# Layer 0 of a two-layer convolution kernel: half-row means from the wave sums, the base bank moved out by ScalarE, the virtual-row product as four tiles

## The chip, the cores and the metric

One core of one Trainium2 chip. The time is device microseconds of one execution, from the first instruction to the last with what lies around them. The kernel before took 4186.73 us in the median of three runs (4180.75 to 4187.25).

## The reference

The input x is (8, 16, 512, 512) in float32. Two layers follow one another.

```python
# layer 0
x = x + irfft2(conv3x3_complex(rfft2(group_norm(x))) + bias)   # 16 -> 16 channels, over the spectrum
# layer 1
x = x + box15x15(group_norm(x))                                # mean filter, per channel
```

The group norm takes mean and variance over two channels of one image (8 groups, eps 1e-5). A 3x3 convolution over a half spectrum becomes, back in the image domain, products of pointwise waves (cosine and sine of the column and of the row), channel mixes, and a term for the edge of the half spectrum, which is a Hilbert transform along the row. The kernel computes layer 0 in that form.

## The kernel before

The kernel works on one image after another (a hardware loop over seven, the eighth written behind it). An image lies in SBUF as `img`, 128 partitions (16 channels by 8 row blocks) by T = 64 rows of 512 columns. One *slot* handles one of the 64 rows `t`; the running row number over all images is `n`. Even and odd columns are two halves `a` of 256 (the parity); a bank of PSUM holds both halves.

Layer 0 of an image, slot by slot, four engines in a pipeline, each with its own program order and semaphores between them. SyncE only fetches the mixing matrices of a later row (`bd_all`, `wrap_mat`) once `p0_ready` says that their buffer is free. The rotation is over NG = 4 rows (`s`).

- **TensorE (PE)**, in slot n: `front_hilbert(n + 1)` (12 matmuls, printed as L442), `front_turn(n + 2)` (8 transposes, L432), `mix(n)`. `mix` runs 36 matmuls of 64x64 tiles by 512 columns (L557) in ten rounds. Row half 0 and row half 1 of the array work on different banks at the same time: `p1`, `p0[s]`, `p2`. In the first and the tenth round only one half of the array has work. Then comes one full 128x128 matmul by 512 columns into `p0[s]`, the virtual rows (`wrap_mat`, L601), whose end is `p0_ready`. Before `mix`, PE waits for `t1_done` of the row before (bank `p1` read), before round 1 for `t2_done`, before round 3 for `x1_done` of row n - 4 (bank `p0[s]` read).
- **ScalarE (ACT)**, in slot n: `normalise(n + 3)` in two instructions (L719 in f16, L720 in f32 into the single buffer `g32`), which waits for `p0_ready` of row n - 1; `keep_hilbert(n + 1)` (L734); `keep_turned(n + 2)` (L726); `add_half_row(n - 3)`: two instructions on 128x1 (L741) make the half-row correction `half_row` from `stat` and `known`, two on 128x256 (L747) add it to the row in place. Its end is `x1_whole`.
- **VectorE (DVE)**, in slot n: `wave_terms(n - 1)`, four SCALAR_TENSOR_TENSOR on 128x256, two from `p1` (L1065) and two from `p2` (L1071), each bank by a wave table into `term_row`; `low_hilbert(n + 1)` (L1038), which waits for ACT's L734; `finish_row(n - 2)`: one SCALAR_TENSOR_TENSOR from bank `p0[s]` and `q_row` into `img` (L1080), then BATCH_NORM_STATS of the row (L1083).
- **GpSimd (POOL)**, in slot n: `split_g(n + 3)` (L1194), which waits for ACT's L720; `add_terms(n - 1)`: L1201 adds the two wave terms, L1203 adds the old row, giving `q_row`. All three read two SBUF operands of 512 columns. In the slots 5 to 11 and 61 to 63 of an image `presum` adds one row more (L1214, L1217) for the box filter of layer 1; it waits for `x1_whole`. Four more presums follow the last row.

Why there is a half-row correction: the Hilbert term of a row leaves open the mean of its even and of its odd columns. The kernel before computes these means beforehand (`known`, from `kappa`, `block_mat`, `vmean`, `from_virtual`) in the head of layer 0 (L1027 to L1056 on DVE, L530 to L533 on PE), compares them with the means that BATCH_NORM_STATS finds, and adds half of the difference. At the end of the loop L1108 mends the statistics in the same way, and only then does `statistics` (L939) begin.

The head of layer 0 (lines 984 to 1056 on DVE) also makes `wrap_row` (L1043), the moving operand of the matmul of L601. It is ready at about the time when the first `mix` has done its 36 matmuls.

Layer 1 (the box filter) and the statistics of the next image follow; the change does not touch them.

## Time and profile before

| | |
|---|---|
| profiled execution, device time | 4181.21 us |
| its span | 4179.4 us |
| median of three runs | 4186.73 us |
| granted TensorE clock, mean | 0.954 |
| busy over the span | PE 88%, DVE 75%, ACT 63%, POOL 63% |
| chain that ended last, by engine | PE 61%, DVE 11%, POOL 10%, issue 6%, DMA 5%, SP queue 3%, ACT 3% |
| its costliest line | L557 (`mix`), 20% |

Busy times overlap, and a share over the span mixes layer 0 with layer 1. The chain says which engine was last at each step. PE instructions overlap one another, so PE is read by the distance from one start to the next and not by durations. The same holds for DVE: two instructions with no wait between them overlap by about 0.08 us.

### The profile page before, as it was taken

To read this page: it belongs to the slowest core of one execution; us is meant where nothing else is said; L and a number is where in the kernel's file an instruction comes from. 1 tells how busy PE (TensorE), PEld (TensorE's weight loads), DVE (VectorE), ACT (ScalarE), POOL (GpSimd) and SP (SyncE) were. 2 spreads that over 40 slices of the span, in tenths; PEclk is the share of its full clock that TensorE was granted. 3 is DMA by queue.
4 is the path that set the end of the run, shared out by engine and by line. 5 is a ranking of instruction groups with operands and counts; after the bars stand their busy time and mean duration, and the time that the engine had idled before them with its cause. 6 is when DMAs were issued, how large, how long until landed. Compare 5 with 4: busy or idle time off the path is not lost.

```text
span 4179.4 us, 122916 instructions
## 1 busy us (share of the span) xinstructions
PE 3686.3 (88%) x41104; PEld 2617.8 (63%) x41104; DVE 3141.1 (75%) x5894; ACT 2619.4 (63%) x4784; POOL 2633.4 (63%) x2177
## 2 busy tenths in 40 slices
PE   3199898998989989899898997899888998989988
PEld 1166575666756667566665666666575666756667
DVE  8778776787767878678776887778776787767876
ACT  0089822997249962599427993289822997239962
POOL 4078742886628865488546885378842887528865
PEclk8599998999999999999999999999999999999999
DMA  7411165111841128211381114711165111741114
GB/s 160 153 45 51 38 189 149 51 51 39 220 119 50 51 61 234 81 51 52 98 235 41 53 48 131 205 43 51 40 179 157 51 51 36 212 127 51 51 48 137
DMA packets 228317, 406.43 MB, mean 97 GB/s; under 512 B 98144, under 2 KB 173504, under 8 KB 215744
## 3 DMA queue, kind: packets, MB, share of 16 engines
q1 hardware_dynamic: 228032, 402.82, 34.8%
q8 instruction: 156, 2.56, 0.3%
q14 instruction: 129, 1.06, 0.1%
HBM read 255.78 MB, written 146.80 MB: 96 GB/s over the span
## 4 chain that ended last, share of the span: by engine, by line
PE 61%; DVE 11%; POOL 10%; issue 6%; DMA 5%; SPq 3%; ACT 3%; DVEq 0%; POOLq 0%; ACTq 0%
PE p L557 20%; PE h_ps L442 13%; PE h_ps L627 10%; DMA img<-in_x 5%; PE xt_ps L432 4%; PE p L653 4%; POOL ob_all L1201 3%; PE p L480 2%; PE h_ps L557 2%; POOL arena L1194 2%; PE p L601 2%; DVE stat L918 2%; POOL ob_all L1203 2%; POOL arena L1217 2%; DVE ob_all L1132 1%
## 5 line engine op out<-in xcount | busy, mean ns | idle before, releaser
L557 PE MATMUL p<-arena,bd_all 64*64 64x512 f16 x16896 | 1217.7, 379 | 16.8 <-DVE ob_all L1065 8.6
L1194 POOL TENSOR_TENSOR arena<-arena 128x512 f16<-128x512 f32 x512 | 592.9, 1158 | 599.1 <-ACT arena L720 531.4
L557 PEld LDWEIGHTS p<-arena,bd_all 64*64 64x64 f16 x16896 | 607.6, 105 | 386.9 <-issue 186.8
L700 ACT ACTIVATE arena<-h_ps 128x512 f16<-128x512 f32 x512 | 305.8, 597 | 861.7 <-PE h_ps L627 651.3
L1252 POOL TENSOR_TENSOR arena<-img 128x512 f32<-128x512 f32 x392 | 499.3, 1275 | 495.0 <-PE h_ps L627 467.0
L442 PE MATMUL h_ps<-hilbert,arena 128*128 128x256 f16 (+1 forms) x6240 | 781.2, 275 | 30.8 <-DVE arena L1038 21.9
L1203 POOL TENSOR_TENSOR ob_all<-ob_all,img 128x512 f32<-128x512 f32 x512 | 662.8, 1295 | 82.9 <-POOL ob_all L1201 72.9
L442 PEld LDWEIGHTS h_ps<-hilbert,arena 128*128 128x128 f16 x6240 | 610.2, 98 | 164.1 <-issue 24.5
L1201 POOL TENSOR_TENSOR ob_all<-ob_all 128x512 f32<-128x512 f32 x512 | 654.5, 1278 | 26.3 <-DVE ob_all L1071 26.3
L1038 DVE SCALAR_TENSOR_TENSOR arena<-h_ps,arena 128x512 f16<-128x512 f32 x512 | 354.0, 691 | 385.8 <-ACT arena L734 384.9
L627 PE MATMUL h_ps<-bd_all,arena 128*128 128x128 f32 x3584 | 543.1, 287 | 0.0
L627 PEld LDWEIGHTS h_ps<-bd_all,arena 128*128 128x128 f32 x3584 | 450.8, 192 | 122.1 <-issue 114.6
L747 ACT ACTIVATE img<-img,half_row (+1 forms) x1024 | 486.3, 526 | 62.2
L726 ACT ACTIVATE arena<-xt_ps 128x1024 f16<-128x1024 f16 x512 | 517.8, 1011 | 1.7 <-PE xt_ps L432 1.7
L719 ACT ACTIVATE arena<-img,sc 128x512 f16 (+1 forms) x512 | 442.3, 864 | 95.4 <-POOL arena L1194 29.5
L1116 DVE TENSOR_TENSOR arena<-h_ps,arena 128x512 f16<-128x512 f32 x512 | 352.8, 689 | 183.2 <-ACT arena L700 178.4
L1065 DVE SCALAR_TENSOR_TENSOR ob_all<-p,bias_c,cosw 128x256 f32<-128x256 f32 x1024 | 441.9, 473 | 11.2 <-PE p L557 10.8
L1071 DVE SCALAR_TENSOR_TENSOR ob_all<-p,bias_c,cosw 128x256 f32<-128x256 f32 x1024 | 443.7, 475 | 0.0
L720 ACT ACTIVATE arena<-img,sc 128x512 f32 (+1 forms) x512 | 433.3, 846 | 0.0
L480 PE MATMUL p<-img,bd_all 128*64 128x256 f32 x2048 | 325.7, 426 | 114.1 <-DMA img<-in_x 63.8
L653 PE MATMUL p<-band,arena 128*128 128x135 f16 (+1 forms) x4096 | 334.3, 225 | 79.6 <-DVE ob_all L1132 77.6
L1083 DVE BATCH_NORM_STATS2 stat<-img (+1 forms) x512 | 355.4, 694 | 62.0
(156 smaller groups left out, 4461.2 us busy)
## 6 DMA issues: line engine op xcount, KB each, us to landing
out<-ob_all SPq DMA_DIRECT2D x512, 256.0 KB, 3.2
img<-in_x SPq DMA_DIRECT2D x192, 512.0 KB, 6.4
bd_all<-bd_dram SPq DMA_DIRECT2D x512, 192.0 KB, 2.2
img<-in_x SPq DMA_DIRECT2D x128, 256.0 KB, 4.6
wrap_mat<-tab_wrap_h SPq DMA_DIRECT2D x512, 32.0 KB, 2.0
bd_dram<-ob_all SPq DMA_DIRECT2D x16, 768.0 KB, 3.5
arena<-tab_hilbert_kernel SPq DMA_DIRECT2D x8, 256.0 KB, 3.3
hilbert<-tab_hilbert SPq DMA_DIRECT2D x1, 522.0 KB, 4.0
```

What stands on the lines that cost most here:

```text
L442: m = mm(dst(a), xT[:, 4 * lx + k, 0:rows], tb["hilbert16"][:, lt, k, 0:cols], start=(half == 0 and i == 0), stop=(half == 1 and i == 2))
L557: m = mm(bank[out_half * HP:(out_half + 1) * HP, :], low(half, 6 * lm + (j if own else j + 1)), (g_part if own else h_part)(half, lp), sta ...
L627: m = mm(turned_ps[u % 2][:, k, :], row[:, k * P:(k + 1) * P], mat, start=(i == 0), stop=(i == len(terms) - 1))
L653: m = mm(p0[0][:, lo:hi], parts[u % 2][:, l, k, :], tb["band16"][:, lo - k * P + R:hi - k * P + R], start=(u == 0 and k == 0 and l == 0), ...
L719: nc.scalar.activation(halves(gp[s][:, 0, :]), row, ACT.Identity, bias=sc[:, 9:10], scale=sc[:, 8:9])
L726: nc.scalar.activation(xT.rearrange("p k (s m) -> p k s m", s=2)[:, :, ::-1, :], xt_ps[:].rearrange("p k (s m) -> p k s m", s=2), ACT.Iden ...
L747: ins = nc.scalar.activation(row, row, ACT.Identity, bias=half_row[:, s, a:a + 1])
L1071: ins = V.scalar_tensor_tensor(t2[:, a, :], p2[:, a * HALF:(a + 1) * HALF], bias_c[:, 0, t, 1 - a:2 - a], sinw[:, a, :], ALU.add, ALU.mult)
L1194: G.tensor_tensor(gp[s][:, 1, :], g32, gp[s][:, 0, :], ALU.subtract).then_inc(g_split, 1)
L1201: G.tensor_tensor(q, term_row[s % 2][0], term_row[s % 2][1], ALU.add).then_inc(t_added, 1)
L1203: G.tensor_tensor(q, q, parity(img[:, t, :]), ALU.add).then_inc(q_done, 1)
L1252: G.tensor_tensor(diff[u % 2], img[:, u + R, :], img[:, u - R - 1, :], ALU.subtract).then_inc(moved, 1)
```

## The change

- `mix` is put in another order. Row half 0 does `p0[s]`, then `p1`, then `p2`; row half 1 does `p1`, `p2`, `p0[s]`. The 128x128 matmul of the virtual rows becomes four 64x64 tiles (`wrap_terms`): two in round 3 on row half 0, two in round 9 on row half 1. There are now ten rounds of four matmuls and nothing behind them. The wait for the bank `p0[s]` stands at the start of `mix` (on `base_done`), the one for `t2_done` before round 3, the one for `v_wrap` (only in the first row) before round 3.
- The four wave instructions on DVE also write their sums along the row (`accum_out`, into `wave_sum`). A new function `half_sums` makes `half_mean` from them in two TENSOR_SCALAR on 128x1, in SBUF from SBUF; DVE does it behind `low_hilbert`.
- ACT does not touch the finished row any more. `keep_base(n - 2)`, now the first thing in its slot, moves bank `p0[s]` with scale and `half_mean` as bias into `base_row` in SBUF (two instructions on 128x256), waiting for `p0_ready`, `half_made` and `x1_done`.
- `finish_row` on DVE adds `q_row` and `base_row`, both in SBUF, by TENSOR_TENSOR, where it read PSUM before.
- `known`, `vmean`, `vwrap`, `half_row`, the table `from_virtual`, a third of `block_mat` and `c_tab`, the waits on them and the correction L1108 are gone. `presum` waits for `x1_done`.

```diff
+        base_row = [piece[8 + s].rearrange("p (a j) -> p a j", a=2) for s in range(2)]
...
-        block_mat = sb("block_mat", [P, 9, P])
+        block_mat = sb("block_mat", [P, 6, P])
         kappa = sb("kappa", [P, 3, T, 2])
         bias_c = sb("bias_c", [P, 2, T, 2])
-        known = sb("known", [P, T, 2])
-        half_row = sb("half_row", [P, NG, 2])
-        vmean = sb("vmean", [NV, 2])
-        vwrap = sb("vwrap", [P, 3, 2])
+        wave_sum = sb("wave_sum", [P, NG, 2, 2])
+        half_mean = sb("half_mean", [P, NG, 2])
...
-                pe.wait_ge(v_means, b + 1)
-                for j in range(3):
-                    m = mm(c_ps[:, 40 + 2 * j:42 + 2 * j], tb["from_virtual"][:, j, :], vmean[:], start=True, stop=True)
-                m.then_inc(v_meant, 1)
...
                     pe.wait_ge(t1_done, PRIMED + n)
+                    if first > 0:
+                        pe.wait_ge(base_done, PRIMED + n - (NG - 1))
                     pe.sem_inc(mix_step, 1)
-                    first_half = [(p1[:], 2)] * 3 + [(p0[s], 0)] * 3 + [(p2[:], 4)] * 3
+
+                    def wrap_terms(half, closes):
+                        for out_half in (half, 1 - half):
+                            m = mm(p0[s][out_half * HP:(out_half + 1) * HP, :],
+                                   wrap_mat[s][half * HP:(half + 1) * HP, out_half * HP:(out_half + 1) * HP],
+                                   wrap_row[half * HP:(half + 1) * HP, :], start=False, stop=closes,
+                                   skip_group_check=True)
+                        return m
                     for r in range(10):
-                        if r == 1:
-                            pe.wait_ge(t2_done, PRIMED + n)
-                            pe.sem_inc(mix_step, 1)
-                        if r == 3 and first > 0:
-                            pe.wait_ge(x1_done, PRIMED + n - (NG - 1))
-                            pe.sem_inc(mix_step, 1)
-                        if r < 9:
-                            bank, j = first_half[r]
-                            if r == 6:
-                                pe.wait_ge(p2_half, n + 1)
+                        if r < 3:
+                            m = half_terms(p0[s], 0, r, 0, True, False)
+                        elif r == 3:
+                            if first == 0 and s == 0:
+                                pe.wait_ge(v_wrap, b + 1)
                                 pe.sem_inc(mix_step, 1)
-                            m = half_terms(bank, j, r % 3, 0, r < 6, r >= 6)
-                            if r == 2:
-                                m.then_inc(p1_half, 1)
-                            if r == 5:
-                                m.then_inc(p0_half, 1)
-                            if r == 8:
-                                m.then_inc(p2_ready, 1)
-                        if r >= 1:
-                            bank, j = first_half[(r + 5) % 9]
+                            wrap_terms(0, False).then_inc(p0_half, 1)
+                        elif r < 7:
                             if r == 4:
                                 pe.wait_ge(p1_half, n + 1)
                                 pe.sem_inc(mix_step, 1)
+                            m = half_terms(p1[:], 2, r - 4, 0, False, True)
+                            if r == 6:
+                                m.then_inc(p1_ready, 1)
+                        else:
                             if r == 7:
+                                pe.wait_ge(p2_half, n + 1)
+                                pe.sem_inc(mix_step, 1)
+                            m = half_terms(p2[:], 4, r - 7, 0, False, True)
+                            if r == 9:
+                                m.then_inc(p2_ready, 1)
+                        if r < 3:
+                            m = half_terms(p1[:], 2, r, 1, True, False)
+                            if r == 2:
+                                m.then_inc(p1_half, 1)
+                        elif r < 6:
+                            if r == 3:
+                                pe.wait_ge(t2_done, PRIMED + n)
+                                pe.sem_inc(mix_step, 1)
+                            m = half_terms(p2[:], 4, r - 3, 1, True, False)
+                            if r == 5:
+                                m.then_inc(p2_half, 1)
+                        elif r < 9:
+                            if r == 6:
                                 pe.wait_ge(p0_half, n + 1)
                                 pe.sem_inc(mix_step, 1)
-                            m = half_terms(bank, j, (r - 1) % 3, 1, r <= 3, r > 3)
-                            if r == 3:
-                                m.then_inc(p2_half, 1)
-                            if r == 6:
-                                m.then_inc(p1_ready, 1)
-                    if first == 0 and s == 0:
-                        pe.wait_ge(v_wrap, b + 1)
-                    mm(p0[s], wrap_mat[s][:], wrap_row[:], start=False, stop=True, skip_group_check=True).then_inc(p0_ready, 1)
+                            half_terms(p0[s], 0, r - 6, 1, False, False)
+                        else:
+                            wrap_terms(1, True).then_inc(p0_ready, 1)
...
-                    if s == NG - 1:
-                        pe.wait_ge(known_made, b + 1)
...
-                def add_half_row(n, t, s):
-
-                    act.wait_ge(x1_counted, n + 1)
+                def keep_base(n, s):
+
+                    act.wait_ge(p0_ready, PRIMED + n + 1)
+                    act.wait_ge(half_made, n + 1)
+                    act.wait_ge(x1_done, PRIMED + n - 1)
                     for a in range(2):
-                        ins = nc.scalar.activation(half_row[:, s, a:a + 1], stat[:, t, 1 + 3 * a:2 + 3 * a], ACT.Identity,
-                                                   bias=known[:, t, a:a + 1], scale=-0.5)
-                    ins.then_inc(half_made, 1)
-                    act.wait_ge(half_made, n + 1)
-                    for a in range(2):
-                        row = img[:, t, a:W:2]
-                        ins = nc.scalar.activation(row, row, ACT.Identity, bias=half_row[:, s, a:a + 1])
-                    ins.then_inc(x1_whole, 1)
+                        ins = nc.scalar.activation(base_row[s % 2][:, a, :], p0[s][:, a * HALF:(a + 1) * HALF],
+                                                   ACT.Identity, bias=half_mean[:, s, a:a + 1], scale=unscale)
+                    ins.then_inc(base_done, 1)
...
+                    if t >= 2:
+                        keep_base(n - 2, (s + 2) % NG)
...
-                    if t >= 3:
-                        add_half_row(n - 3, i * NG + s - 3, (s + 1) % NG)
...
-                dve.wait_ge(v_rows, b + 1)
-                lk(V.tensor_reduce(vmean[:], vrow[0:NV], mybir.AxisListType.X, ALU.add))
-                V.tensor_scalar(vmean[:], vmean[:], 1.0 / HALF, None, ALU.mult).then_inc(v_means, 1)
                 dve.wait_ge(c_made, b + 1)
-                V.tensor_copy(bias_c[:], c_tab[:, 0:2])
-                lk(V.scalar_tensor_tensor(known[:], c_tab[:, 2], unscale, parity_mean, ALU.mult, ALU.add))
-                V.scalar_tensor_tensor(known[:, 0, 0:1], bcol[:, 0:1], 1.0 / HALF, known[:, 0, 0:1],
-                                       ALU.mult, ALU.add).then_inc(c_kept, 1)
+                V.tensor_copy(bias_c[:], c_tab).then_inc(c_kept, 1)
...
-                dve.wait_ge(v_meant, b + 1)
                 dve.wait_ge(c_kept, b + 1)
-                lk(V.tensor_copy(vwrap[:].rearrange("p j a -> p (j a)"), c_ps[:, 40:46]))
-                for f in range(2):
-                    for a in range(2):
-                        ins = V.scalar_tensor_tensor(known[:, :, a], tb["trig_h"][:, f], vwrap[:, 1 + f, a:a + 1],
-                                                     known[:, :, a], ALU.mult, ALU.add)
-                    lk(ins)
-                for a in range(2):
-                    ins = V.tensor_scalar(known[:, :, a], known[:, :, a], vwrap[:, 0, a:a + 1], 0.5, ALU.add, ALU.mult)
-                ins.then_inc(known_made, 1)
-                dve.wait_ge(known_made, b + 1)
...
                         ins = V.scalar_tensor_tensor(t1[:, a, :], p1[:, a * HALF:(a + 1) * HALF],
                                                      bias_c[:, 1, t, 1 - a:2 - a], cosw[:, a, :],
-                                                     ALU.subtract, ALU.mult)
+                                                     ALU.subtract, ALU.mult, accum_out=wave_sum[:, s, 0, a:a + 1])
...
-                                                     ALU.add, ALU.mult)
+                                                     ALU.add, ALU.mult, accum_out=wave_sum[:, s, 1, a:a + 1])
...
+                def half_sums(n, s):
+
+                    dve.wait_ge(t1_done, PRIMED + n + 1)
+                    dve.wait_ge(t2_done, PRIMED + n + 1)
+                    for a in range(2):
+                        ins = V.tensor_scalar(half_mean[:, s, a:a + 1], wave_sum[:, s, 0, a:a + 1],
+                                              wave_sum[:, s, 1, a:a + 1], -0.5 / HALF, ALU.add, ALU.mult)
+                    ins.then_inc(half_made, 1)
+
+                def finish_row(n, t, s):
 
                     dve.wait_ge(q_done, PRIMED + n + 1)
-                    dve.wait_ge(p0_ready, PRIMED + n + 1)
-                    V.scalar_tensor_tensor(parity(img[:, t, :]), halves(p0[s]), unscale, q_row[s % 2],
-                                           ALU.mult, ALU.add).then_inc(x1_done, 1)
+                    dve.wait_ge(base_done, PRIMED + n + 1)
+                    V.tensor_tensor(parity(img[:, t, :]), q_row[s % 2], base_row[s % 2], ALU.add).then_inc(x1_done, 1)
...
+                    if t >= 1:
+                        half_sums(n - 1, (s - 1) % NG)
                     if t >= 2:
-                        finish_row(n - 2, i * NG + s - 2, (s - 2) % NG, first - (s < 2))
+                        finish_row(n - 2, i * NG + s - 2, (s - 2) % NG)
...
-                for t in (T - 2, T - 1):
-                    finish_row(b * T + t, t, t % NG, T // NG)
-                dve.wait_ge(half_made, (b + 1) * T)
-                V.scalar_tensor_tensor(parity_mean, parity_mean, 0.5, known[:], ALU.mult, ALU.add).then_inc(stat_fixed, 1)
-                dve.wait_ge(stat_fixed, b + 1)
+                half_sums(b * T + T - 1, (T - 1) % NG)
+                for t in range(T - 2, T):
+                    finish_row(b * T + t, t, t % NG)
+                dve.wait_ge(x1_counted, (b + 1) * T)
                 statistics(b * 2 + 2, b)
...
-                    pool.wait_ge(x1_whole, n + 1)
+                    pool.wait_ge(x1_done, PRIMED + n + 1)
```

## Rows read from the trace of the kernel before

**Rows 1.** Windows: one stretch of the loop of layer 0, second image; window, length, busy time.

```profile
787.50:1000.10 212.60, 212.33 (x2694) 142.85 (x2691) 171.89 (x334) 203.53 (x378) 175.58 (x144) 1.00 0.18 51
```

**Rows 2.** Timeline: PE in one slot; start us, duration us, engine, line.

```profile
867.79 0.39 PE L601 MATMUL p<-wrap_row,wrap_mat 128*128 128x512 f16 x1
868.02 1.48 PE L442 MATMUL h_ps<-hilbert,arena 128*128 128x256 f16 x12
...
869.88 2.47 PE L557 MATMUL p<-arena,bd_all 64*64 64x512 f16 x36
...
872.28 0.39 PE L601 MATMUL p<-wrap_row,wrap_mat 128*128 128x512 f16 x1
```

**Rows 3.** Timeline: DVE in the same slot.

```profile
868.22 0.88 DVE L1065 SCALAR_TENSOR_TENSOR ob_all<-p,bias_c,cosw 128x256 f32<-128x256 f32 x2
...
869.01 0.87 DVE L1071 SCALAR_TENSOR_TENSOR ob_all<-p,bias_c,cosw 128x256 f32<-128x256 f32 x2
...
870.54 0.69 DVE L1038 SCALAR_TENSOR_TENSOR arena<-h_ps,arena 128x512 f16<-128x512 f32 x1 [0.67 <-ACT arena L734]
...
871.15 0.74 DVE L1080 SCALAR_TENSOR_TENSOR img<-p,sc,ob_all 128x512 f32 x1
...
872.04 0.69 DVE L1083 BATCH_NORM_STATS2 stat<-img  x1
...
872.65 0.86 DVE L1065 SCALAR_TENSOR_TENSOR ob_all<-p,bias_c,cosw 128x256 f32<-128x256 f32 x2
```

**Rows 4.** Timeline: ACT's `add_half_row` in the loop, and `virtual_base` in the head.

```profile
866.81 0.48 ACT L741 ACTIVATE half_row<-stat,known 128x1 f32 x2
...
867.43 0.95 ACT L747 ACTIVATE img<-img,half_row  x2
```
```profile
714.89 1.02 ACT L755 ACTIVATE ob_all<-p,edge,sc 128x256 f32<-128x256 f32 x2 [3.62 <-DVE edge L1016]
```

**Rows 5.** Timeline: POOL in the same slot.

```profile
870.11 1.16 POOL L1194 TENSOR_TENSOR arena<-arena 128x512 f16<-128x512 f32 x1 [0.62 <-ACT arena L720]
...
871.23 1.28 POOL L1201 TENSOR_TENSOR ob_all<-ob_all 128x512 f32<-128x512 f32 x1
...
872.70 1.29 POOL L1203 TENSOR_TENSOR ob_all<-ob_all,img 128x512 f32<-128x512 f32 x1 [0.19 <-POOL ob_all L1201]
```

**Rows 6.** Timeline: two small DVE instructions, no wait between them.

```profile
696.62 0.14 DVE L966 TENSOR_SCALAR sc<-sc 128x1 f32<-128x1 f32 x1
696.68 0.14 DVE L967 TENSOR_SCALAR sc<-sc 128x1 f32<-128x1 f32 x1
```

**Rows 7.** Timeline: DVE and POOL in the setup, then one DVE instruction behind layer 0.

```profile
27.42 1.22 DVE L310 TENSOR_TENSOR img<-img 128x1024 f32<-128x1024 f32 x1
...
33.83 3.25 DVE L308 TENSOR_TENSOR img<-img 128x1024 f32<-128x1024 f32 x1
```
```profile
32.68 3.33 POOL L308 TENSOR_TENSOR img<-img 128x1024 f32<-128x1024 f32 x1
```
```profile
1025.37 1.23 DVE L1138 TENSOR_SCALAR mean_in<-c_mask,sc 128x16 f32<-128x16 f32 x1
```

**Rows 8.** Timeline: POOL in two slots with a presum; starts of `mix` of rows 2 and 15.

```profile
754.65 1.29 POOL L1203 TENSOR_TENSOR ob_all<-ob_all,img 128x512 f32<-128x512 f32 x1
...
759.61 1.30 POOL L1203 TENSOR_TENSOR ob_all<-ob_all,img 128x512 f32<-128x512 f32 x1
```
```profile
733.55 2.47 PE L557 MATMUL p<-arena,bd_all 64*64 64x512 f16 x36
```
```profile
793.54 2.47 PE L557 MATMUL p<-arena,bd_all 64*64 64x512 f16 x36
```

**Rows 9.** Timeline: PE's two waits in the head of layer 0.

```profile
720.29 1.48 PE L442 MATMUL h_ps<-hilbert,arena 128*128 128x256 f16 x12 [0.67 <-DVE arena L1038]
...
727.21 1.48 PE L442 MATMUL h_ps<-hilbert,arena 128*128 128x256 f16 x12 [2.08 <-DVE arena L1038]
```

**Rows 10.** Timeline: DVE's last correction of layer 0.

```profile
1017.20 0.69 DVE L1108 SCALAR_TENSOR_TENSOR stat<-stat,known 128x128 f32<-128x128 f32 x1 [0.55 <-ACT half_row L741]
```

29 lines of the change are left out of this document (12 added, 17 removed).

## The prediction

> **What bounds the kernel now.** I read the chain that ended last first (the table ahead): PE 61%, its costliest line the mix. Then the windows: over 212.60 us of the loop of layer 0 PE is busy for 212.33, ACT for 203.53, POOL for 175.58 and DVE for 171.89 [rows 1]. So inside layer 0 PE sets the pace, and ACT is hardly behind. Then the timeline of one slot. PE's rows abut: from one L601 to the next are 4.49 us (867.79 to 872.28), and no PE row carries a wait [rows 2]. Eight images of 64 slots make 512 slots, so 0.01 us of a slot are 5 us of the time.
>
> DVE has to be read by starts. L1065 takes 0.79 us to the next start, L1071 the same (two of one kind), L1038 0.61 (870.54 to 871.15), L1080 0.89 with the gap behind it (871.15 to 872.04), L1083 0.61 (872.04 to 872.65): 3.69 us, and 0.67 us of the slot it waits for ACT's L734 [rows 3]. POOL has L1194, L1201, a gap of 0.19 and L1203, 3.88 us, and waits 0.62 for ACT [rows 5].
>
> **The change, part by part.**
>
> *The virtual-row product.* L601 takes 0.23 us of PE to the next start (867.79 to 868.02) [rows 2]. Its four tiles fill the empty places of rounds 0 and 9. The ten rounds stay (869.88 to 872.28 is 2.40 us, with the hand-over to the 128x128 array), so the slot becomes 4.49 - 0.23 = 4.26 us. Bounds: 0.23 gained, or nothing, if 40 matmuls take 40/36 of 2.40 us (0.27 more). I take the gain: round by round the array streams 512 columns, and a round with two matmuls does not start its successor sooner than one with four. In slots 2 to 63: 62 x 0.23 = 14.3 us per image. The price is that every other engine must do its slot in 4.26.
>
> *ACT.* The 128x1 pair L741 and the gap behind it go (0.62 us, 866.81 to 867.43), the pair L747 goes (0.95), and a pair from PSUM comes, between 0.95 (L747) and 1.02 us (L755) [rows 4]. ACT had 203.53/212.60 x 4.49 = 4.30 us of work and gets about 3.7 (3.9 with the gap counted). It fits. `keep_base` stands ahead of `normalise`, which PE and POOL wait for, but in the time in which ACT would wait for `p0_ready` of the row before. Its own wait, `half_made`, comes from DVE behind L1038; that is the one place where DVE can now hold up ACT.
>
> *DVE.* Out: L1080 from PSUM, 0.74. In: TENSOR_TENSOR of two SBUF rows, 0.69 by L1083's and L1038's length [rows 3], -0.05. Four accumulator outputs: no row shows one. Below, they cost nothing; above, one small instruction each with its whole 0.14 us (0.56). I take 0.06 each, the distance of small instructions with no wait [rows 6], 0.24. `half_sums`: two such, 0.13. Sum 3.69 - 0.05 + 0.24 + 0.13 = 4.01 of 4.26. It fits, with 0.25 us left, where it had 0.80.
>
> *The SBUF reads of DVE and POOL.* This is the part that the diff does not show. Now no DVE instruction of the slot has two full rows of 512 columns from SBUF while POOL runs [rows 3]. The setup shows what happens then. L310 on 128x1024 takes 1.22 us alone. L308, the same instruction, takes 3.25 (33.83 to 37.08) while POOL's L308 runs from 32.68 to 36.01; 36.01 + 1.07 (1024 columns at 1.22 us less start-up) is 37.08, to the hundredth [rows 7]. So DVE stood until POOL's instruction had ended. The Trainium skill says so too ("SBUF — State Buffer", "Who interferes with whom": two SBUF inputs on VectorE against a GpSimd read, an exclusive lock), and the trace agrees. The new TENSOR_TENSOR on 512 columns holds the reads for half of 1.07, 0.53 us, and waits for whatever POOL is in, 0 to 1.2 us. POOL's 3.88 becomes at worst 4.41; where DVE falls into POOL's own gap of 0.19 or its wait for ACT (0.27 of a 4.26 us slot), POOL loses less than 0.4 and stays within 4.26. DVE can wait at most 0.25 us before it sets the pace. I take it that the two settle in step, DVE in POOL's pauses, since each one that comes late is then met by a pause: 4.26 us. The other case is a rival.
>
> *Presums.* In their seven slots POOL needs 4.96 us (754.65 to 759.61). PE loses only 1.6 us to that now: rows 2 to 15 are 59.99 us apart, against 13 x 4.49 = 58.37 [rows 8]. Wanted were 7 x 0.47 = 3.3; a reserve of 1.7 covered the rest. After: 4.96 + 0.53 = 5.49 against 4.26, 7 x 1.23 = 8.6, less the reserve, 6.9. That gives back 5.3; with POOL's thinner reserve in faster slots I take 6.5.
>
> *Head.* PE waits 0.67 and 2.08 us for L1038, which stands behind the work on `known` [rows 9]. That work is gone. The new wait for `v_wrap` before round 3 costs PE about 1.9 us in row 0, as `wrap_row` is ready only when the 36 matmuls are done, but PE had 2.08 to wait there. The next Hilbert matmuls follow that mix at once. From the chain of starts: 0.9 us at each place, -1.8.
>
> *Tail.* L1108 and the wait for L741 ahead of it go: 0.69 + 0.55 = -1.2 [rows 10]. But the last TENSOR_TENSOR meets POOL's presums (+1 us), as do the small two-operand instructions of the statistics (+0.5), and POOL itself comes 0.5 later. +0.8 in sum, between -1.2 and +2.
>
> *Setup* is 1 us shorter (three of nine block matrices, one table). The SP queue waits for `p0_ready` as before.
>
> **Sum** per image: -14.3 + 6.5 - 1.8 + 0.8 = -8.8; I round the doubtful give-back up to -7.8. Eight images: -62, and the setup: 4181.2 - 63 = 4118 us for an execution like the profiled one. The median of the runs lies 5.5 above that one and the lowest 0.5 below, so the median may read as much higher: 4120.
>
> **The rivals.**
>
> *H, the two 128x1 instructions are held too (slower).* `half_sums` is TENSOR_SCALAR from SBUF to SBUF with one tensor operand. Such an instruction can be held as well: L1138, 128x16, takes 1.23 us beside a POOL instruction, where a small one takes 0.14 [rows 6, 7]. For it: same kind, same place. Against it: no row shows a 128x1 one beside POOL, so one element may be too few for the mode that does it. If it holds, DVE stands for one whole POOL instruction between the first and the second (POOL's next is already waiting), about 1.1 us of 1.27 [rows 5]: 4.01 + 1.1 = 5.1 us a slot, against 4.49 now. It decides as soon as the held time is over 0.25 us. 62 x 0.6 = 37, presum slots +2, head and tail -1: +38 x 8 = +305, 4490 us (4440 to 4560). The Trainium skill ("Vector Engine (DVE) Microarchitecture Reference", "5.1 Performance modes") lets an odd count use both ports if source and destination match; by that rule one element would be held, and this rival is right. No row here shows it. 35%.
>
> *M, DVE and POOL do not settle.* TENSOR_TENSOR is met by a running POOL instruction for half of its 1.2 us in each slot. 4.01 + 0.6 = 4.6 us a slot: 62 x 0.11 = 7, presums +3, head and tail -1, +9 per image: 4181 + 72 = 4253 (4215 to 4300). The same comes of accumulator outputs at 0.14 each (4.33 before any hold). For it: only 0.25 us of slack. Against it: POOL has pauses of 0.46 us in a slot. 13%.
>
> *S, no change.* The gain of the rounds is not there (40 matmuls for 36), or a slot of about 4.45 by DVE. 5%.
>
> **How the numbers follow.** Forecast F, DVE in step with POOL: 47%. Own range: the rounds at 0.20 to 0.23, the give-back of the presums at 5.3 to 8.5, the tail from -1.2 to +2: -4 to -12 per image, 4085 to 4150. Cases of both signs hold most of the chance, so the range for 8 in 10 reaches from 4085 through M and S into H, up to 4500: some 6 in 10 of H, the 47% less a little, 13 and 5, together 83%. About 0.2% (8 us) is what a measurement of this kernel can tell from no change. Faster: F and a little of S, 49%. Within: 4%. Slower: M and H, 47%.
>
> **What would show it.** Right: L557 rows in the loop 4.26 us apart with no L601 behind them; `half_sums` rows of 0.14 us; the TENSOR_TENSOR of `finish_row` at 0.69 to 1.0 us; ACT with waits. H: rows of `half_sums` with a mean near 1 us, PE with waits for DVE in each slot, starts of the mix 5.1 apart. M: the `finish_row` row above 1.2 us and slots of 4.6. In the slots with presums a distance of about 5.5 in each case. The forecast is wrong if DVE's slot, holds included, is over 4.49.

## The result and the profile after

The changed kernel takes 4286.66 us in the median of four runs (4284.46 to 4287.94), the kernel before 4183.74 beside it on the same chip (4178.26 to 4187.25): a ratio of 1.0247, with a 95% interval of 1.0229 to 1.0264. It is slower by 103 us. The forecast was 4120. The range, 4085 to 4500, holds the time, but the time moved the other way than the likeliest case had it.

The page of the profile after: busy times and the chain that ended last, then groups of instructions (line, engine, operation, tiles, count | busy us, mean ns | idle before, releaser).

```profile
PE 3671.1 (86%) x42544; PEld 2504.6 (58%) x42544; DVE 3563.4 (83%) x8867; ACT 2465.9 (58%) x3760; POOL 2770.6 (65%) x2177
...
DVE 30%; PE 30%; issue 15%; POOL 7%; ACT 6%; DMA 5%; SPq 3%; DVEq 3%; ACTq 0%; POOLq 0%
...
L548 PE MATMUL p<-arena,bd_all 64*64 64x512 f16 x16896 | 1343.0, 382 | 113.2 <-DVE ob_all L1048 61.4
...
L1195 POOL TENSOR_TENSOR ob_all<-ob_all,img 128x512 f32<-128x512 f32 x512 | 760.3, 1485 | 82.9 <-POOL ob_all L1193 72.9
```

PE's share of the chain fell from 61% to 30%, DVE's rose from 11% to 30%. PE idles 113 us ahead of the matmuls of `mix` (L548 now), more than half of it for the wave terms of DVE. POOL's L1195 takes 1485 ns in the mean, where L1203 took 1.29 us [rows 5].

The groups of instructions of DVE alone show the new instructions:

```profile
L1072 DVE TENSOR_TENSOR img<-ob_all,arena 128x512 f32 (+1 forms) x512 | 701.8, 1371 | 3.5 <-POOL ob_all L1195 3.5
L1032 DVE SCALAR_TENSOR_TENSOR arena<-h_ps,arena 128x512 f16<-128x512 f32 x512 | 352.5, 689 | 76.9 <-ACT arena L737 66.4
L1064 DVE TENSOR_SCALAR half_mean<-wave_sum 128x1 f32<-128x1 f32 x1024 | 166.5, 204 | 1.7
```

L1072 is `finish_row` with both operands in SBUF: 1371 ns in the mean, where a DVE row of 512 columns takes 0.69 us [rows 3]. That is 0.68 us of standing, 512 times, on an engine that had 0.25 us to spare in the forecast. By the start times of the trace each of the 512 began inside an instruction of POOL, 417 of them inside L1193. L1064 is `half_sums`: 204 ns each, so it is not held by POOL.

The windows answer over the stretch of [rows 1], and over 42 slots without a presum; then the same 42 slots, L1072 alone (window, length, busy us of PE, PEld, DVE, ACT and POOL, clock, DMA share, GB/s):

```profile
787.50:1000.10 212.60, 200.08 (x2680) 125.43 (x2676) 202.12 (x584) 181.17 (x271) 179.85 (x138) 1.00 0.18 49
806.00:1004.10 198.10, 187.91 (x2522) 117.96 (x2520) 189.63 (x547) 169.36 (x254) 165.00 (x127) 1.00 0.18 49
806.00:1004.10 198.10, 58.44 (x42) 1.00 0.18 49
```

A slot is 198.10 / 42 = 4.72 us. L1072 takes 58.44 / 42 = 1.39 of it.

The timeline of DVE and of POOL behind it (start us, duration us; the accumulator reads of DVE, which lie beside the waves, are left out):

```profile
1007.33 0.69 DVE L1074 BATCH_NORM_STATS2 stat<-img  x1
1007.94 0.47 DVE L1048 SCALAR_TENSOR_TENSOR ob_all<-p,bias_c,cosw 128x256 f32<-128x256 f32 x1
...
1008.33 0.48 DVE L1048 SCALAR_TENSOR_TENSOR ob_all<-p,bias_c,cosw 128x256 f32<-128x256 f32 x1
...
1009.55 0.69 DVE L1032 SCALAR_TENSOR_TENSOR arena<-h_ps,arena 128x512 f16<-128x512 f32 x1
1010.15 0.33 DVE L1064 TENSOR_SCALAR half_mean<-wave_sum 128x1 f32<-128x1 f32 x2
1010.39 1.24 DVE L1072 TENSOR_TENSOR img<-ob_all,arena 128x512 f32 x1
1011.78 0.69 DVE L1074 BATCH_NORM_STATS2 stat<-img  x1
...
1014.88 1.65 DVE L1072 TENSOR_TENSOR img<-ob_all,arena 128x512 f32 x1
1016.67 0.69 DVE L1074 BATCH_NORM_STATS2 stat<-img  x1
```
```profile
1014.71 1.27 POOL L1193 TENSOR_TENSOR ob_all<-ob_all 128x512 f32<-128x512 f32 x1
1016.17 1.51 POOL L1195 TENSOR_TENSOR ob_all<-ob_all,img 128x512 f32<-128x512 f32 x1 [0.19 <-POOL ob_all L1193]
```

From 1007.33 to 1011.78, 4.45 us, DVE's instructions follow one another with no pause but the 0.15 behind L1072, whose result L1074 reads. L1072 took 1.24 there; unheld (0.69) the same list would take 3.90 us. In the next slot L1072 starts at 1014.88, 0.17 us behind POOL's L1193. That ends at 1015.98, and L1072 ends at 1016.53, 0.55 us later: the same reading as in the setup [rows 7], with 0.53 for 512 columns. With the mean L1072, DVE's list is 3.90 + 1.39 - 0.69 = 4.60 us of the slot of 4.72. The rest, 0.12, is waiting in single slots: of the 42, DVE pauses ahead of L1032 in 12 and ahead of the first wave in 11. PE in turn stands ahead of `mix` in 20 of them, 10.2 us in sum (0.42 us at 1018.40, for DVE's L1048), and that is most of what its slot grew over the 4.44 us that experiment 2 will show.

### The profile page after: what moved, and what is told of

Its sections match the earlier page's. It is cut to its first block, busy times and chain, and to the rows that moved or that the text cites. A ratio compares the mean times of both kernels' runs of the same rounds, so it can differ in the third digit from the quotient of the medians.

```text
span 4282.6 us, 126110 instructions
## 1 busy us (share of the span) xinstructions
PE 3671.1 (86%) x42544; PEld 2504.6 (58%) x42544; DVE 3563.4 (83%) x8867; ACT 2465.9 (58%) x3760; POOL 2770.6 (65%) x2177
## 4 chain that ended last, share of the span: by engine, by line
DVE 30%; PE 30%; issue 15%; POOL 7%; ACT 6%; DMA 5%; SPq 3%; DVEq 3%; ACTq 0%; POOLq 0%
DVE img L1072 10%; PE h_ps L630 10%; PE p L548 8%; DMA img<-in_x 5%; DVE ob_all L1054 4%; DVE ob_all L1048 4%; PE p L656 4%; PE h_ps L437 2%; PE p L475 2%; DVE half_mean L1064 2%; POOL ob_all L1193 2%; DVE stat L918 2%; POOL arena L1186 2%; POOL arena L1209 2%; ACT arena L722 2%
## 5 line engine op out<-in xcount | busy, mean ns | idle before, releaser
L548 PE MATMUL p<-arena,bd_all 64*64 64x512 f16 x16896 | 1343.0, 382 | 113.2 <-DVE ob_all L1048 61.4
L1186 POOL TENSOR_TENSOR arena<-arena 128x512 f16<-128x512 f32 x512 | 612.1, 1196 | 575.6 <-ACT arena L723 508.2
L548 PEld LDWEIGHTS p<-arena,bd_all 64*64 64x64 f16 x16896 | 536.3, 105 | 616.7 <-issue 426.6
L1195 POOL TENSOR_TENSOR ob_all<-ob_all,img 128x512 f32<-128x512 f32 x512 | 760.3, 1485 | 82.9 <-POOL ob_all L1193 72.9
L437 PEld LDWEIGHTS h_ps<-hilbert,arena 128*128 128x128 f16 x6240 | 569.6, 98 | 291.9 <-issue 190.0
L1072 DVE TENSOR_TENSOR img<-ob_all,arena 128x512 f32 (+1 forms) x512 | 701.8, 1371 | 3.5 <-POOL ob_all L1195 3.5
L1193 POOL TENSOR_TENSOR ob_all<-ob_all 128x512 f32<-128x512 f32 x512 | 670.8, 1310 | 23.4 <-DVE ob_all L1054 20.5
L1108 DVE TENSOR_TENSOR arena<-h_ps,arena 128x512 f16<-128x512 f32 x512 | 352.8, 689 | 181.8 <-ACT arena L703 177.2
L746 ACT ACTIVATE arena<-p,half_mean,sc 128x256 f32<-128x256 f32 x768 | 392.0, 560 | 159.2 <-DVE half_mean L1064 73.2
L1048 DVE SCALAR_TENSOR_TENSOR ob_all<-p,bias_c,cosw 128x256 f32<-128x256 f32 x1024 | 448.3, 475 | 17.4 <-PE p L548 9.6
L1054 DVE SCALAR_TENSOR_TENSOR ob_all<-p,bias_c,cosw 128x256 f32<-128x256 f32 x1024 | 452.6, 479 | 0.0
L723 ACT ACTIVATE arena<-img,sc 128x512 f32 (+1 forms) x512 | 435.2, 850 | 0.0
L1032 DVE SCALAR_TENSOR_TENSOR arena<-h_ps,arena 128x512 f16<-128x512 f32 x512 | 352.5, 689 | 76.9 <-ACT arena L737 66.4
L1074 DVE BATCH_NORM_STATS2 stat<-img (+1 forms) x512 | 355.4, 694 | 62.2
```

What stands on the lines that cost most here:

```text
L437: m = mm(dst(a), xT[:, 4 * lx + k, 0:rows], tb["hilbert16"][:, lt, k, 0:cols], start=(half == 0 and i == 0), stop=(half == 1 and i == 2))
L548: m = mm(bank[out_half * HP:(out_half + 1) * HP, :], low(half, 6 * lm + (j if own else j + 1)), (g_part if own else h_part)(half, lp), sta ...
L1048: ins = V.scalar_tensor_tensor(t1[:, a, :], p1[:, a * HALF:(a + 1) * HALF], bias_c[:, 1, t, 1 - a:2 - a], cosw[:, a, :], ALU.subtract, ALU ...
L1054: ins = V.scalar_tensor_tensor(t2[:, a, :], p2[:, a * HALF:(a + 1) * HALF], bias_c[:, 0, t, 1 - a:2 - a], sinw[:, a, :], ALU.add, ALU.mult ...
L1072: V.tensor_tensor(parity(img[:, t, :]), q_row[s % 2], base_row[s % 2], ALU.add).then_inc(x1_done, 1)
L1186: G.tensor_tensor(gp[s][:, 1, :], g32, gp[s][:, 0, :], ALU.subtract).then_inc(g_split, 1)
```

## The experiments

Eleven kernels ran, each beside the kernel before, whose medians were 4181.02 us (experiments 1 to 4), 4187.42 (5 to 8) and 4185.09 (9 to 11). A ratio is to that median. The medians lie 6 us apart, so differences of that size between the groups say little. The letters in the expectations (C, D, P, R, W, I, H') name theories that are explained where they stand; this H' is not the rival H of the prediction.

**1. Read the finish from PSUM, leave all else of the change** (`e1_psum_read`).

```diff
-                        pe.wait_ge(base_done, PRIMED + n - (NG - 1))
+                        pe.wait_ge(x1_done, PRIMED + n - (NG - 1))
...
-                    V.tensor_tensor(parity(img[:, t, :]), q_row[s % 2], base_row[s % 2], ALU.add).then_inc(x1_done, 1)
+                    V.scalar_tensor_tensor(parity(img[:, t, :]), halves(p0[s]), unscale, q_row[s % 2],
+                                           ALU.mult, ALU.add).then_inc(x1_done, 1)
```

> Leaves the half means out of the output; ACT still makes base_row with all its waits, but finish_row on DVE reads bank p0 from PSUM again (SCALAR_TENSOR_TENSOR with q_row), and PE waits for x1_done for that bank. Theory C (DVE's TENSOR_TENSOR of two SBUF rows is held by POOL, 0.68 us a slot in the mean): the hold goes, DVE's slot is 1.62 + 0.61 + 0.24 + 0.89 + 0.61 = 3.97 us, PE sets the pace at 4.26, and the time is 4080 to 4110 us. Rival D (the rest of DVE's new work, or ACT's wait for half_mean, makes the slot long): the slot stays at 4.6 or more and the time at 4230 or more.

Measured: 4142.17 us (4141.06 to 4143.39), ratio 0.9907 (0.9891 to 0.9924). This version leaves the half means out of its output, though it still makes them. One instruction's operand moved from SBUF to PSUM takes 144 us off the changed kernel and puts it below the one before. All other parts of the change, ACT's `keep_base`, `half_sums`, the accumulator outputs and the new `mix`, are still there. So together they cost no time, and the slow-down lies in this read. Theory C was right about the hold and wrong in the time (4080 to 4110): PE's slot is 4.43 us and not 4.26.

**2. The half-row mean, made in place in PSUM** (`e2_in_place`). ACT writes scale times the bank plus `half_mean` back into the same bank, and DVE adds it to `q_row` from there.

```diff
-                    act.wait_ge(x1_done, PRIMED + n - 1)
...
-                        ins = nc.scalar.activation(base_row[s % 2][:, a, :], p0[s][:, a * HALF:(a + 1) * HALF],
+                        ins = nc.scalar.activation(p0[s][:, a * HALF:(a + 1) * HALF], p0[s][:, a * HALF:(a + 1) * HALF],
...
-                    V.tensor_tensor(parity(img[:, t, :]), q_row[s % 2], base_row[s % 2], ALU.add).then_inc(x1_done, 1)
+                    V.tensor_tensor(parity(img[:, t, :]), halves(p0[s]), q_row[s % 2], ALU.add).then_inc(x1_done, 1)
```

> ACT writes the scaled base with the half mean back into its own PSUM bank instead of into SBUF; finish_row adds that bank and q_row by TENSOR_TENSOR, so one operand only is in SBUF; PE waits for x1_done for the bank. Theory C: as e1, 4080 to 4110 us, faster than both kernels, with L1072 near 0.75 us and POOL's adds at 1.3. Rival D: 4230 or more. Rival P (ACT's write and DVE's read in one bank disturb each other or PE): L1072 or ACT's pair is longer than 0.75 and 1.02 us.

Measured: 4140.81 us (4138.38 to 4142.96), ratio 0.9902 (0.9886 to 0.9919). It computes the whole output and is, with experiment 7, the fastest kernel of the study, 1% below the one before and 3.4% below the change. Rival P is refuted: L1070 takes 0.68 us. The timeline of its DVE and PE, one slot:

```profile
854.08 0.69 DVE L1030 SCALAR_TENSOR_TENSOR arena<-h_ps,arena 128x512 f16<-128x512 f32 x1 [0.47 <-ACT arena L736]
854.68 0.33 DVE L1062 TENSOR_SCALAR half_mean<-wave_sum 128x1 f32<-128x1 f32 x2
854.92 0.68 DVE L1070 TENSOR_TENSOR img<-h_ps,ob_all 128x512 f32 x1
855.75 0.69 DVE L1072 BATCH_NORM_STATS2 stat<-img  x1
```
```profile
853.50 0.84 PE L547 MATMUL p<-arena,bd_all 64*64 64x512 f16 x12
...
856.07 1.49 PE L436 MATMUL h_ps<-hilbert,arena 128*128 128x256 f16 x12
...
857.94 0.84 PE L547 MATMUL p<-arena,bd_all 64*64 64x512 f16 x12
```

The same TENSOR_TENSOR of 512 columns takes 0.68 us once one operand is in PSUM, although POOL is in L1191 at that time (854.76 to 856.03 in its own rows), and DVE waits for ACT again. PE abuts, with a slot of 4.44 (853.50 to 857.94). From the start of `mix` to the Hilbert matmuls it takes 2.57 us, against 2.63 before (869.88 to 872.28, and 0.23 for L601) [rows 2]. So the new `mix` saves 0.06 us a slot, not 0.23.

**3. Only the new `mix` in the kernel before** (`e3_tiles_only`): the order of the banks, the four tiles and the places of the waits as in the diff ahead, `known` and the correction of rows as before.

```diff
-                        if r == 1:
-                            pe.wait_ge(t2_done, PRIMED + n)
...
-                    first_half = [(p1[:], 2)] * 3 + [(p0[s], 0)] * 3 + [(p2[:], 4)] * 3
...
+                            wrap_terms(0, False).then_inc(p0_half, 1)
...
```

> The kernel before with the new order of mix alone (the virtual rows as tiles, the wait for bank p0 at the start). If the four tiles take the empty places, PE's slot is 4.26, but ACT has 4.30 to 4.46 us of work with add_half_row, so the slot is 4.3 to 4.46 and the time 4110 to 4170 us. If 40 matmuls take 40/36 of the time of 36, no change or slower: 4185 to 4210.

Measured: 4158.47 us (4155.95 to 4162.39), ratio 0.9948 (0.9932 to 0.9965), a slot of 4.44. This part of the change, alone, is a gain of 0.5%, some 22 us, where the forecast gave it 8 x 14.3 = 114 less what the presums take back. The time lies in the range expected (4110 to 4170) for another reason than the one expected: from 790 to 990 us PE is busy for all 200.00 us and ACT for 193.96, so the slot is PE's own and not ACT's.

**4. Only the rest: the change with the old `mix`** (`e4_no_tiles`): the 36 matmuls in the old order, the wait for `t2_done` before round 1 instead of round 3, and L601's 128x128 matmul behind them.

```diff
+                        if r == 1:
+                            pe.wait_ge(t2_done, PRIMED + n)
...
+                    mm(p0[s], wrap_mat[s][:], wrap_row[:], start=False, stop=True, skip_group_check=True).then_inc(p0_ready, 1)
```

> The kernel after with the old order of mix and the 128x128 matmul of the virtual rows, all else as after. Theory C: DVE with its holds sets the pace at about 4.73 us a slot whatever PE does below that, so the time stays within 10 us of 4287, less 0 to 10 where the first mix of an image no longer waits for wrap_row. If PE still counts, it is slower by up to 62 x 0.23 x 8 = 114 us: 4400.

Measured: 4406.94 us (4403.85 to 4409.49), ratio 1.0538 (1.052 to 1.0555): 120 us more than the change, with a slot of 5.04 in rows 15 to 60. A slot bound by DVE alone would not have moved, as theory C had it; the measured time is 7 us above the 4400 of "if PE still counts". The groups of DVE, then the timelines of DVE and PE over two slots, then PE's waits, first here and then in the change (us in total, times, longest):

```profile
L1058 DVE TENSOR_TENSOR img<-ob_all,arena 128x512 f32 (+1 forms) x512 | 714.5, 1395 | 3.6 <-POOL ob_all L1181 3.6
L1018 DVE SCALAR_TENSOR_TENSOR arena<-h_ps,arena 128x512 f16<-128x512 f32 x512 | 352.6, 689 | 184.0 <-ACT arena L723 184.0
```
```profile
872.83 0.69 DVE L1018 SCALAR_TENSOR_TENSOR arena<-h_ps,arena 128x512 f16<-128x512 f32 x1 [0.70 <-ACT arena L723]
...
873.68 1.65 DVE L1058 TENSOR_TENSOR img<-ob_all,arena 128x512 f32 x1
...
882.83 0.69 DVE L1018 SCALAR_TENSOR_TENSOR arena<-h_ps,arena 128x512 f16<-128x512 f32 x1 [0.55 <-ACT arena L723]
```
```profile
877.21 0.40 PE L548 MATMUL p<-arena,bd_all 64*64 64x512 f16 x2 [0.45 <-DVE ob_all L1034]
877.91 2.25 PE L548 MATMUL p<-arena,bd_all 64*64 64x512 f16 x34 [0.30 <-DVE ob_all L1040]
```
```profile
PE p L548 <- DVE ob_all L1034: 112.1, 233, 1.1
...
PE p L548 <- DVE ob_all L1040: 86.8, 256, 0.4
```
```profile
PE p L548 <- DVE ob_all L1048: 61.4, 119, 0.9
...
PE p L548 <- issue: 49.5, 106, 1.7
```

The held time is nearly what it was (1395 ns against 1371). What grew is DVE's wait for ACT's Hilbert copy: 184.0 us against 66.4, 117.6 of the 120. Since DVE's work is the same in both, this says where the time shows and not what made it. PE says more. It stands 199 us ahead of `mix` for DVE's waves, of which 87 are for t2 (L1040); in the change it stands some 120 (the 111 of the two rows, and 9 where the bank carries another name), none for t2. These 79 us and the longer `mix` (2.63 us for 2.57, 31 us in 512) are 110 of the 120. The rows tell how the waits follow one another: a late DVE makes PE wait for t1 and t2 (0.45 and 0.30 at 877), the late `mix` makes the next Hilbert product late, and DVE waits 0.55 for it at 882.83. So the two engines stand in a ring over two slots, and what a held instruction takes comes back in part. That is read from the rows: this experiment changes the order of `mix` and the place of the wait for `t2_done` together, and no run moves the wait alone.

**5. The change without accumulator outputs** (`e5_no_accum`).

```diff
-                                                     ALU.subtract, ALU.mult, accum_out=wave_sum[:, s, 0, a:a + 1])
+                                                     ALU.subtract, ALU.mult)
```

> The kernel after without the four accumulator outputs (wave_sum is set to zero once, so the output lacks the half means). The trace of after shows an accumulator read of 0.08 us beside each wave instruction, but the starts of these are 0.40 us apart where they were 0.395. If the outputs cost next to nothing: 4287 less 0 to 20 us. If each took 0.06 us or more of DVE, the time falls by 60 us or more (0.24 x 62 x 8 = 119, or half of that where the ring of two slots decides).

Measured: 4278.82 us, ratio 1.022 (1.0203 to 1.0237), 8 us below the change, as expected of outputs that cost next to nothing. In the trace after, the starts of the waves are 0.40 us apart (1007.94, 1008.33, 1008.74), where L1065's pairs took 0.79 to the next start [rows 3]. The instruction that reads the accumulator (L1048 DVE_READ_ACCUMULATOR, 83 ns) lies beside the next wave. Over 42 slots the four waves with outputs take 0.05 us more to the start of `low_hilbert` than the four without, 0.01 each. Not all of that shows in the time, as `finish_row` stood longer here (1408 ns in the mean, for 1371).

**6. Finish ahead of `low_hilbert` in DVE's program** (`e6_finish_first`), all else as in the change.

```diff
+                    if t >= 2:
+                        finish_row(n - 2, i * NG + s - 2, (s - 2) % NG)
                     if t + 1 < T:
                         low_hilbert(n + 1, (s + 1) % NG)
...
-                    if t >= 2:
-                        finish_row(n - 2, i * NG + s - 2, (s - 2) % NG)
```

> The kernel after, all parts in, but DVE does finish_row(n - 2) ahead of low_hilbert(n + 1) and half_sums(n - 1). Theory R (a ring over two slots sets the pace: end of mix, ACT's normalise and L737, DVE's low_hilbert, half_sums, the held TENSOR_TENSOR, statistics, waves, the next mix): the held instruction leaves the ring, and DVE's own sum of about 4.59 us or PE's 4.43 decides: 4140 to 4240 us. Theory C alone (DVE's sum of instructions with the hold is the pace, in any order): within 15 us of 4287.

Measured: 4249.15 us (4247.34 to 4250.22), ratio 1.0148 (1.0131 to 1.0165), 37 us below the change. Theory R missed by 9 us (4140 to 4240), theory C by more (within 15 us of 4287).

```profile
852.90 0.69 DVE L1072 TENSOR_TENSOR img<-ob_all,arena 128x512 f32 x1 [0.59 <-POOL ob_all L1195]
...
857.47 0.69 DVE L1072 TENSOR_TENSOR img<-ob_all,arena 128x512 f32 x1 [0.59 <-POOL ob_all L1195]
```

The hold is gone in these slots, as L1072 now starts just when POOL has ended L1195: 424 of its 512 instances begin with POOL idle, and these take 693 ns in the mean. But it starts then because it waits for that instruction's result, 0.59 us. One wait on POOL took the place of the other, at a slot of 4.57. This is what "DVE in POOL's pauses" looks like where it happens, and it is dearer than PE's slot too.

**7 and 8. The in-place version with another queue order.** `e7_lower_first` issues row half 1 first in rounds 4 and 7, so that it does not stand behind half 0's wait in PE's queue. `e8_both` adds the DVE order of experiment 6.

```diff
+                    for r in range(10):
+                        for part in ((lower, upper) if r in (4, 7) else (upper, lower)):
+                            part(r)
```

> e2 (bank written in place) with one more edit on PE: in rounds 4 and 7 of mix, where row half 0 waits for a bank that half 1 has filled, the two matmuls of half 1 are issued ahead of that wait. In e3 rounds 0 to 3 start 0.22 us apart and round 9 starts 2.25 us after round 0, 0.33 later than nine times 0.213. Theory W (the waits between the halves hold up PE's queue): the slot falls from 4.43 to 4.2 to 4.35 us, 4060 to 4110. Theory I (PE issues 40 matmuls and 40 weight loads no faster): 4141 within 8 us.

> e7 and the order of e6 on DVE. If PE sets the pace in e7, this changes nothing (within 10 us of e7). If DVE or the ring is near, it is up to 30 us faster; if finish_row now waits for POOL's q_row, slower.

Measured: 4141.63 us (4140.97 to 4143.65; ratio 0.9893, 0.9877 to 0.991) for the first, as without it: theory I held, W (4060 to 4110) did not. 4175.98 (4169.65 to 4183.04; ratio 0.9974, 0.9963 to 0.9984) for the second, 34 us more: unheld in either order, `finish_row` only gained the wait for `q_row` (286 us in sum, where experiment 7 has 12). So PE's missing 0.17 us is not a matter of which half stands first in its queue.

**9, 10 and 11. What sets the length of `mix`.** All three start from the in-place version. `e9_nine_rounds` leaves the four virtual-row tiles out (9 rounds), `e10_eleven_rounds` issues them twice (11 rounds), and `e11_in_place_old_mix` has the old `mix`.

```diff
-                    for r in range(10):
+                    for r in range(9):
...
-                            if r == 4:
+                            if r == 3 + 0:
                                 pe.wait_ge(p1_half, n + 1)
```

> The version with the sum made in place, without the four tiles of the virtual row in each mix: 9 rounds of four tiles instead of 10 (36 instead of 40). It leaves out the virtual rows' terms, in every mix. Theory I (the mix lasts as long as its count of tiles, 2.40 us for 40): 4 tiles fewer are 0.24 us a slot, so 4.43 - 0.24 = 4.19 us in 1008 slots' image pairs as they stand: about 62 slots x 0.24 = 15 us would be the gain if a slot were an image, and it is 512 / 8 = 64 images of 8 slots, so up to 120 us where PE alone bounds the slot (4020 to 4060 us; the sum of DVE is 4.0 to 4.2, which may stop it near 4050). Theory H' (the mix is paced by the handing of a bank from one row half of the tiles to the other, with some 0.5 us from the last tile of the one to the first of the other): the handings stand as close as before, the slot stays at 4.40 to 4.43, and the time within 15 us of 4141.

> The version with the sum made in place, with the four tiles of the virtual row issued twice: 11 rounds (44 tiles), with two rounds between the two halves of bank p1 and of p0 where there was one. It adds the virtual rows' terms twice, in every mix. Theory I: 4 tiles more are 0.24 us a slot, about 4260 us. Theory H': the added round only fills the time of the handings; the slot stays at 4.43 to 4.50 and the time at 4141 to 4180 us.

> The version with the sum made in place, with the mix as it was in the kernel before (9 rounds and 128 x 128 matmul of the virtual row behind them). It computes the whole output. Where a slot is bound by PE with 0.06 us more in the mix (2.63 against 2.57 from its start to the Hilbert transform's), 512 slots x 0.06 = 30 us more than with the tiles: 4165 to 4180 us. A rival: the wait for t2, one round or two earlier here, closes a ring over ACT and DVE as it did where the finish read two SBUF operands (0.24 us a slot); then about 4260 us.

Measured: 4379.66 us for 36 tiles (ratio 1.0471, 1.0437 to 1.0505), 4140.81 for 40, and 4166.7 for 44 (4164.52 to 4170.72; 0.996, 0.9948 to 0.9972). Fewer matmuls took 239 us longer. Both theories missed that by far. Theory I fails in both directions. H' held for eleven rounds, and for nine it had the right place but had left out that the hand-over would be laid bare. The timeline of PE with nine rounds, a narrower window of it, then ten rounds (experiment 2):

```profile
854.51 0.84 PE L547 MATMUL p<-arena,bd_all 64*64 64x512 f16 x12
855.54 2.12 PE L547 MATMUL p<-arena,bd_all 64*64 64x512 f16 x24 [0.19 <-PE p L547]
857.59 1.49 PE L436 MATMUL h_ps<-hilbert,arena 128*128 128x256 f16 x12
```
```profile
854.97 0.39 PE L547 MATMUL p<-arena,bd_all 64*64 64x512 f16 x4
...
855.54 0.55 PE L547 MATMUL p<-arena,bd_all 64*64 64x512 f16 x4 [0.19 <-PE p L547]
```
```profile
809.38 0.38 PE L547 MATMUL p<-arena,bd_all 64*64 64x512 f16 x2
...
809.60 0.38 PE L547 MATMUL p<-arena,bd_all 64*64 64x512 f16 x2
809.81 0.38 PE L561 MATMUL h_ps<-wrap_row,wrap_mat 64*64 64x512 f16 x2
...
810.60 0.38 PE L547 MATMUL h_ps<-arena,bd_all 64*64 64x512 f16 x2
810.93 0.40 PE L547 MATMUL p<-arena,bd_all 64*64 64x512 f16 x2
```

Rounds start 0.21 to 0.22 us apart (809.38, 809.60, 809.81). A bank that goes from one row half to the other waits for a semaphore that the last matmul of the first half raises at its end. In the nine-round version nothing stands between: the third round starts at 854.97, the fourth at 855.54, 0.57 us on instead of 0.22, with PE idle for 0.19. The other row half follows another 0.15 later (the four matmuls from 855.54 on take 0.55 us, four that start together 0.39). There are two such places, and `mix` takes 3.08 us instead of 2.57. With ten rounds one round lies between, and the places show as 0.33 instead of 0.22, as from 810.60 to 810.93. An eleventh round filled them further: `mix` took 2.62 us from its start to the Hilbert matmuls, 0.05 more for four more tiles.

The old `mix` in the in-place version: 4191.71 us (4181.7 to 4196.78), ratio 1.0018 (1.0004 to 1.0032), 51 us above experiment 2, where 24 to 39 were expected; the rival's 4260 did not come either. In the slots without a presum it is 4.56 us a slot against 4.44. Of these 0.12, 0.06 are the length of `mix`. The rest lies in single slots in which round 1 waits for `t2_done` (one slot in four is 4.73 us long instead of some 4.5). So the moved wait looks like a gain of its own, though no run moves it alone. And the rework of the half means, free of the held read, gains nothing with the old `mix`: 4192 against 4185.

## Why the prediction failed, step by step

**The step that failed** is "I take it that the two settle in step, DVE in POOL's pauses". The contention itself was seen and priced: 0.53 us of reading and the wait for POOL's instruction, as in the setup [rows 7]. Its mean, 0.68 us, lies inside "0 to 1.2 us" and near the 0.6 of rival M. What was wrong is that the engines would find the cheap phase. They don't, and both sides of the meeting hang on ACT. POOL's L1186 waits for ACT's L723, and L1193 stands right behind it. ACT's next instruction, L737, is what `low_hilbert` needs, and `half_sums` and L1072 stand right behind that:

```profile
1013.42 0.57 ACT L737 ACTIVATE arena<-h_ps 128x512 f16<-128x512 f32 x1
```
```profile
1013.59 1.16 POOL L1186 TENSOR_TENSOR arena<-arena 128x512 f16<-128x512 f32 x1 [0.81 <-ACT arena L723]
```

So L1193 begins at 1014.71 and L1072 at 1014.88, inside it. Where DVE is later against POOL (1010.39, with L1193 from 1009.82) it still falls inside. POOL's pauses, ahead of L1186 and between L1193 and L1195, lie elsewhere in the slot. DVE's list became 4.60 us where 4.26 was allowed. Rival M, at 13%, gave 4253 (4215 to 4300) at a slot of 4.6; the run is 4287 at 4.72. M priced DVE's list nearly right, and the 0.12 us of waiting came on top. The rows of experiment 4 suggest that an uneven DVE brings these waits on itself through PE; no run takes them by themselves.

**PE's gain** was mis-sized: 0.23 us a slot foretold, 0.06 measured. "The ten rounds stay" held for their number and not for their length. In the kernel before, the 2.40 us were 2.07 from the first round to the last and 0.33 from there to a full-array matmul, as the slot behind that of [rows 2] shows:

```profile
874.37 0.91 PE L557 MATMUL p<-arena,bd_all 64*64 64x512 f16 x12
...
876.44 0.41 PE L557 MATMUL h_ps<-arena,bd_all 64*64 64x512 f16 x2
876.77 0.39 PE L601 MATMUL h_ps<-wrap_row,wrap_mat 128*128 128x512 f16 x1
```

The switch to the full array stays, in front of the Hilbert matmuls (0.31 us from the last tile's start). The new order spends 2.25 us on its rounds (853.50 to 855.75 in experiment 2), 0.18 more than the old. The bare number of hand-overs does not explain this: the old order too has two with a single round between (bank `p1` from round 2 to 4, `p0[s]` from round 5 to 7). Why its rounds go faster stays open; the two halves run about 0.1 us out of step there (rounds at 870.12 and 870.34 on one, 870.03 and 870.27 on the other), and no experiment takes that by itself. So even with no hold at all the time stays above the 4120 of the forecast; experiment 2 shows what was there, 4141, which is still inside "4085 to 4150".

**Accumulator outputs**: taken at 0.06 us each, measured at 0.01. **`half_sums`**: taken at 0.13 for the pair, measured at 0.24 (1010.15 to 1010.39). The two errors cancel in part, and DVE's unheld list of 3.90 us is near the 4.01 foretold.

**Rival H**, at 35%, is refuted: 1024 instructions of 128x1 take 204 ns in the mean and at most 215, and POOL is busy beside each of them (the pair of 1014.64 stands where POOL goes from L1186 to L1193). By the trace, TENSOR_SCALAR on 128x1 is free beside POOL. The prediction had concluded otherwise from the Trainium skill ("Vector Engine (DVE) Microarchitecture Reference", "5.1 Performance modes"). That section allows the mode with both ports for an odd count of equal source and destination, and it counts the outermost dimension that is longer than one; it does not say what becomes of a single element, so it neither carried the conclusion nor is it contradicted here. The rule of the Trainium skill on two SBUF inputs ("SBUF — State Buffer", "Who interferes with whom") agrees with the trace: 1.37 us for L1072, against 0.68 with an operand in PSUM.

**Presums**: slots of about 5.5 were foretold, and L1072's starts there are 5.36 to 5.42 us apart (776.91, 782.30, 787.69, 793.11, 798.47):

```profile
776.91 1.26 DVE L1072 TENSOR_TENSOR img<-ob_all,arena 128x512 f32 x1
...
798.47 1.27 DVE L1072 TENSOR_TENSOR img<-ob_all,arena 128x512 f32 x1
```

**Head**: the wait of the four tiles for `wrap_row` was foretold at about 1.9 us and is there with 1.84:

```profile
734.10 0.40 PE L562 MATMUL p<-wrap_row,wrap_mat 64*64 64x512 f16 x2 [1.84 <-DVE wrap_row L1037]
```

From the first `mix` to the Hilbert matmuls behind it are 4.60 us (731.42 to 736.02), against 5.06 before (722.15 to 727.21) [rows 9]: 0.46 of the 0.9 foretold. At the first place, from the matmuls with `block_mat` to the Hilbert matmuls that waited 0.67, 4.73 us (724.84 to 729.57) stand against 5.45 (714.84 to 720.29): 0.72 of 0.9. The tail was not taken apart.

The sum closes by the starts of `mix`. In the second image rows 15 to 60, 45 slots with no presum, take 212.4 us (806.01 to 1018.40) against 202.1 (793.54 to 995.62): 0.23 a slot. Rows 2 to 15, seven of them with a presum, take 63.7 (742.32 to 806.01) against 60.0 [rows 8], and rows 0 to 2 take 10.9 against 11.4. Over the eight images that is 82, 30 and -4 us; all the rest, tail, layer 1 and setup, is -5 by difference, and together it is the 103. So the stretch with the presums is not nothing: it bears nearly a third.

## What to carry to other kernels

An instruction with two full SBUF operands on VectorE, placed where GpSimd is nearly always busy, should be priced at its held mean (here 0.68 us beside GpSimd instructions of 1.2 to 1.3) and never at the phase one hopes for. Moving one operand to PSUM took the hold away at no cost in time here, with ScalarE writing its result back into the bank that it read. When a matmul disappears from the end of a chain of tiles, measure from start to start what follows it: here the switch to the full array and the hand-overs of banks stayed. And follow a wait between engines over two slots, since a late VectorE may come back to itself through TensorE, as the rows of experiment 4 suggest.
